# All four gate pairs of a fused Mamba and MLP block on ScalarE and GpSimd, weights loaded later, a new table of steps

## What is computed

```
x = x + mamba(layernorm(x))
x = x + mlp(layernorm(x))

mamba: xp, res = split(x @ W_in.T)              # 512 + 512 columns
       xc      = silu(causal_conv4(xp) + conv_b)
       B, C, r = split(xc @ W_x.T)              # 16 + 16 + 1 columns
       dt      = softplus(r @ W_dt.T + b_dt)    # 512 columns
       for t, for each of 16 states n:
           h[n] = exp(-A[n] * dt[t]) * h[n] + dt[t] * xc[t] * B[t, n]
       y[t]    = sum over n of h[n] * C[t, n] + D * xc[t]
       out     = silu(y + res) @ W_out.T
mlp:   h = silu((x @ w1) * s1) * ((x @ w2) * s2)      # 256 -> 1024, the "gate"
       h = gelu((h @ h1) * t1)                        # 1024 -> 1024
       h = gelu((h @ h2) * t2)                        # 1024 -> 1024
       out = (h @ w3) * s3                            # 1024 -> 256
```

## Time and profile before

| | |
|---|---|
| median of 3 runs (lowest, highest) | 2656.89 us (2654.86, 2658.69) |
| the profiled execution: its time, its span | 2656.22 us, 2654.1 us |
| busy: PE, DVE, ACT, POOL | 93%, 87%, 83%, 83% of the span |
| before scan 0 of chunk 0 | 46.7 us |
| body 0, body 1 | 81.8 us, 60.8 us |
| bodies 2 to 30 | 1740.7 us |
| body 31 and the tail up to pass B | 187 us |
| pass B | 537 us |

### The profile page before, as it was taken

One profiled execution on the slowest core, in us unless ns is written; L12 is line 12 of the kernel. 1 busy time (PEld: TensorE's weight loads), 2 busy tenths in 40 slices (PEclk: granted clock), 3 DMA queues, 4 the chain that ended last, 5 costly groups with the idle time before them and its releaser, 6 DMA issues. The chain is left out here.

```text
span 2654.1 us, 54444 instructions
## 1 busy us (share of the span) xinstructions
PE 2463.5 (93%) x18562; PEld 2237.4 (84%) x18562; DVE 2304.3 (87%) x2640; ACT 2207.4 (83%) x5264; POOL 2189.7 (83%) x1372
## 2 busy tenths in 40 slices
PE   3678999999999999999999999999977899999999
PEld 2457888888888888888888888888877899999999
DVE  1899999999999999999999999999990387677686
ACT  4799989998899999999899998999876677777774
POOL 2678999999999999999999999999975576666662
PEclk8789999999999999999999999999988899999999
DMA  6121222222222222232222222222231123222320
GB/s 240 51 63 54 73 81 73 81 77 71 79 77 76 74 76 79 70 88 69 81 73 73 77 73 81 73 81 77 68 124 68 64 96 96 96 85 92 96 96 34
DMA packets 148249, 215.91 MB, mean 81 GB/s; under 512 B 18049, under 2 KB 111361, under 8 KB 147969
## 3 DMA queue, kind: packets, MB, share of 16 engines
q1 hardware_dynamic: 147968, 212.36, 25.4%
HBM read 144.68 MB, written 50.86 MB: 74 GB/s over the span
## 5 line engine op out<-in xcount | busy, mean ns | idle before, releaser
L1499 DVE TENSOR_TENSOR_SCAN h<-banks,ub 128x512 f32<-128x512 f32 x1024 | 1196.6, 1205 | 10.4 <-POOL ub L905 3.5
L1512 DVE SCALAR_TENSOR_TENSOR acc<-banks,c_tok,acc 128x512 f32<-128x512 f32 x1024 | 714.9, 733 | 51.2 <-PE banks L1850 48.1
L1850 PE MATMUL banks<-ident,h 128*128 128x128 f32 x4096 | 623.0, 279 | 97.5 <-DVE acc L1512 51.9
L1850 PEld LDWEIGHTS banks<-ident,h 128*128 128x128 f32 x4096 | 483.5, 143 | 226.3 <-DVE h L1499 113.0
L905 POOL TENSOR_TENSOR ub<-xc_even,b_row 128x1020 f32<-128x1020 f32 x256 | 608.0, 2379 | 75.7 <-DVE h L1499 75.2
L905 POOL TENSOR_TENSOR ub<-xc_odd,b_row 128x1020 f32<-128x1020 f32 x256 | 608.1, 2379 | 53.7 <-DVE h L1499 53.1
L1292 ACT ACTIVATE banks<-dt 128x510 f32<-128x510 f32 x1024 | 607.6, 598 | 50.1 <-DVE h L1499 40.7
L1838 PE MATMUL banks<-act_high,h_rounded 128*128 128x256 f32 x2048 | 536.6, 298 | 22.1 <-POOL act_low L937 22.1
L1838 PE MATMUL banks<-act_low,h_rounded 128*128 128x256 f32 x2048 | 506.3, 283 | 0.0
L1838 PEld LDWEIGHTS banks<-act_high,h_rounded 128*128 128x128 f32 x2048 | 392.6, 192 | 28.3 <-issue 28.2
L1838 PEld LDWEIGHTS banks<-act_low,h_rounded 128*128 128x128 f32 x2048 | 393.2, 192 | 0.0
(11 more groups left out here) (167 smaller groups left out, 5784.3 us busy)
## 6 DMA issues: line engine op xcount, KB each, us to landing
b_row<-b_scratch SPq DMA_DIRECT2D x128, 512.0 KB, 4.0
z_scratch<-z_out SPq DMA_DIRECT2D x128, 256.0 KB, 2.4
zl_raw<-z_scratch SPq DMA_DIRECT2D x32, 1024.0 KB, 7.1
xp<-xp SPq DMA_DIRECT2D x128, 128.0 KB, 2.4
x_sb<-in_x SPq DMA_DIRECT2D x32, 256.0 KB, 4.3
x_res<-in_x SPq DMA_DIRECT2D x32, 256.0 KB, 2.9
h_full<-in_h SPq DMA_DIRECT2D x2, 4096.0 KB, 22.3
x_scratch<-x_sb SPq DMA_DIRECT2D x32, 256.0 KB, 2.1
```

What stands on the lines that cost most here:

```text
L1499: nc.vector.tensor_tensor_scan(h[:, n % 2, 2 * i:2 * i + 2].rearrange("p e t -> p (e t)"), banks[:, k % DECAYS, :], ub[:, n % 2, 2 * i:2 * ...
L1512: nc.vector.scalar_tensor_tensor(out=acc[:, par, q], in0=turned[q], scalar=c_tok[:, par, q, n:n + 1], in1=acc[:, par, q], op0=ALU.mult, op ...
L1850: last = nc.tensor.transpose(turned[q][:, e * P:(e + 1) * P], h[:, n % 2, e, q * P:(q + 1) * P], ident[:])
```

## The change

1. Pairs 1 and 2 of the gate go the way of 0 and 3: `BY_POOL` holds all four, `BY_DVE` none. VectorE has no work in the MLP of pass A any more.
2. SP issues the crossing of chunk 0 ahead of w1 and w2, and that of chunk 1 ahead of h2; w3 goes to step 8 of body 0.
3. Chunk 0: TensorE makes the first quarter of its B rows and the first column of B by products with the identity; VectorE and ScalarE copy them out of PSUM. VectorE does the linear part of dt (in place of ScalarE's relu), copies acc, and makes `ub[0]`. The state that enters chunk 0 is zero, so `enter`, `a_dt` and b0 are not formed there.
4. The tables of places are written anew for all engines, the pieces of checking and rounding weights too.

```diff
-        ACT_AT = dict(sums=11, x1=23, sums2=41, logs=15, logs2=41, xn=30, xp=(0, 2), silu=(6, 25), ssm=13, z=18, soft=21, acc=(28, 29), gT=14, high2=49, gg=(56, 65), high=(58, 64, 69, 69), z_out=(75, 76, 82, 86), a_dt=31)
-        POOL_AT = dict(gate=(29, 33), low2=25, x1=12, normalize=9, normalize2=21, dt=(11, 13), a_dt=15, u=(15, 15), low=(30, 32, 34, 34))
-        SP_AT = dict(crossed=(0, 0), x=0, x1=11, res=11, write_b=5, b=(9, 14, 2, 6), z_out=(36, 37, 40, 42))
+        ACT_AT = dict(sums=11, x1=22, sums2=35, logs=12, logs2=36, xn=30, xp=(0, 2), silu=(8, 25), ssm=9, z=16, soft=19, acc=(30, 30), gT=12, high2=46, gg=(55, 55, 60, 63), high=(58, 62, 63, 68), z_out=(74, 78, 85, 88), a_dt=30)
+        POOL_AT = dict(gate=(29, 29, 31, 33), low2=25, x1=12, normalize=7, normalize2=19, dt=(10, 11), a_dt=12, u=(15, 15), low=(30, 32, 34, 34))
+        SP_AT = dict(crossed=(0, 0), x=0, x1=11, res=11, write_b=4, b=(14, 15, 6, 10), z_out=(36, 38, 41, 43))
-        BY_POOL, BY_DVE = (0, 3), (1, 2)
+        BY_POOL, BY_DVE = (0, 1, 2, 3), ()
...
             load_x(1)
+            for j in range(2):
+                cross(0, j)
             for name, src in (("w1", w1), ("w2", w2)):
                 sp.dma_start(full[name][:], src.rearrange("(k p) n -> p k n", p=P)).then_inc(early_in, 16)
-            for j in range(2):
-                cross(0, j)
             write_b(0)
-            read_b(0, 0)
             read_b(0, 1)
             sp.dma_start(full["h1"][:], h1.rearrange("(k p) n -> p k n", p=P)).then_inc(h1_in, 16)
             load_x(2)
-            for name, src in (("h2", h2), ("w3", w3)):
-                sp.dma_start(full[name][:], src.rearrange("(k p) n -> p k n", p=P)).then_inc(checked_in, 16)
...
                         if n == SP_AT["crossed"][j] and to_front is not None:
                             cross(to_front, j)
+                            if to_front == 1 and j == 1:
+                                sp.dma_start(full["h2"][:], h2.rearrange("(k p) n -> p k n", p=P)).then_inc(checked_in, 16)
+                    if to_front == 1 and n == 8:
+                        sp.dma_start(full["w3"][:], w3.rearrange("(k p) n -> p k n", p=P)).then_inc(checked_in, 16)
...
+                    for e in range(ET):
+                        last = nc.vector.tensor_scalar(dt[:, 0, e], bank("dtc", 0)[:, 0:T], w_dt_sb[:, e:e + 1], b_dt_sb[:, e:e + 1], ALU.mult, ALU.add)
+                    last.then_inc(linear_done, 1)
...
+                    nc.vector.tensor_tensor(ub[:, 0, :, 1:], u[0][:, :, 1:], b_row[:, 0, 0:1, 1:].to_broadcast([P, ET, T - 1]), ALU.mult).then_inc(first_ub, 1)
...
+                            nc.tensor.matmul(turned[0][:, 0:T], select(ROW_B), ssm[:, 0], start=True, stop=True)
```

More of the change, by code:

```diff
@@ L312, in program @@
         PE_AT = dict(
[L313 to L316, removed]
@@ new lines, in program @@
+            front={1: ('conv0', 'conv1'), 5: ('ssm.a', 'ssm.b'), 11: ('dtc',), 21: ('acc0.a',), 23: ('acc0.b', 'acc0.c'), 24: ('acc1.a',), 25: ('acc1.b',), 26: ('acc1.c',)},
+            post={7: ('gT0',), 8: ('gT1',), 12: ('out.a',), 13: ('out.b',), 14: ('out.c',), 15: ('out.d',)},
+            mlp={41: ('yn',), 49: ('gg0.a', 'gg0.b'), 50: ('gg1.a', 'gg1.b'), 51: ('uu0.a', 'uu0.b'), 52: ('uu1.a', 'uu1.b', 'uu2.a'), 53: ('uu2.b', 'uu3.a', 'uu3.b', 'gg2.a'), 57: ('gg2.b',), 59: ('gg3.a', 'gg3.b'), 67: ('h0.a', 'h0.b'), 69: ('h0.c',), 70: ('h0.d',), 71: ('h1.a', 'h1.b'), 73: ('h1.c', 'h1.d'), 74: ('h2.a',), 75: ('h2.b',), 77: ('h2.c',), 79: ('h2.d',), 80: ('h3.a',), 81: ('h3.b',), 83: ('h3.c', 'h3.d')})
@@ L860, in front @@
                         nc.gpsimd.tensor_tensor(dt[:, par, rows], dt[:, par, rows], soft[:, rows], ALU.add).then_inc(dt_ready, 1)
-                if n == POOL_AT["a_dt"]:
-                    if c == 0:
+                if n == POOL_AT["a_dt"] and c >= 1:
+                    if c == 1:
                         pool.wait_ge(a_ready, 2)
@@ L902, in scan @@
                         quarter = n // QUARTER
[L903 to L906 removed]
+                        if c == 0 and quarter == 0:
+                            pool.wait_ge(rows_taken, 1)
+                        else:
+                            pool.wait_ge(b_in[quarter % 2], 16 * (2 * c + quarter // 2 + quarter % 2))
+                    if (c, n) != (0, 0):
+                        after(pool, scan_done, 2 * (NS * c + n - 1))
+                        nc.gpsimd.tensor_tensor(ub[:, n % 2, :, 1:], u[par][:, :, 1:], b_row[:, n // QUARTER % 2, n % QUARTER:n % QUARTER + 1, 1:].to_broadcast([P, ET, T - 1]),
+                                                ALU.mult).then_inc(ub_ready, 1)
                     between(n)
@@ L1130, in front @@
                     last.then_inc(soft_step, 1)
-                if n == ACT_AT["z"] + 1:
+                if n == ACT_AT["z"] + 1 and c == 0:
+                    act.wait_ge(linear_done, 1)
+                    act.sem_inc(freed("dtc", 0), 1)
+                elif n == ACT_AT["z"] + 1:
                     rows = bank("dtc", c)
@@ L1142, in front @@
                 for q in range(NT):
-                    if n == ACT_AT["acc"][q]:
+                    if n == ACT_AT["acc"][q] and c >= 1:
                         if c >= 2:
@@ L1549, in _ @@
             nothing = lambda c, n: None
-            bodies(nothing, front, scan, nothing, mlp, make_diagonals, DVE_STEPS)
+            bodies(nothing, front, scan, nothing, nothing, make_diagonals, DVE_STEPS)
             def split_rows(name, blk):
@@ L1772, in front @@
                         q = int(job[-1])
+                        if c == 0 and q == 1 and part == "a":
+                            nc.tensor.matmul(turned[0][:, 0:T], select(ROW_B), ssm[:, 0], start=True, stop=True)
+                            nc.tensor.matmul(turned[1][:, 0:NS], ssm[:, 0, 0:1].to_broadcast([P, P]), ident[:, ROW_B:ROW_B + NS], start=True, stop=True).then_inc(rows_full, 1)
                         if part != "c":
@@ L1780, in front @@
                             last.then_inc(job_full, 1)
+                            if c == 0 and q == 1:
+                                pe.wait_ge(row0_taken, 2)
+                                for r in range(1, QUARTER):
+                                    last = nc.tensor.matmul(turned[r // 2][:, r % 2 * T:r % 2 * T + T], select(ROW_B + r), ssm[:, 0], start=True, stop=True)
+                                last.then_inc(rows_full, 1)
             def post(c, n):
```

104 lines of the change are left out of this document (62 added, 42 removed).

## The result

The changed kernel takes 2691.1 us (median of 4 runs, 2688.4 to 2697.1) against 2656.7 us for the kernel before (4 runs, 2654.9 to 2658.7): ratio 1.0132, 95% interval 1.0114 to 1.0151. It is slower by 1.3%. The profiled executions have spans of 2690.2 and 2654.1 us, 36.1 apart. Forecast were 2677 us, range 2652 to 2698; the result lies inside this range, and 1 us above the narrower 2666 to 2690 of the forecast itself.

A forecast was written before the change was run, and what follows sets the result against it. VectorE was taken to bound the steady bodies, GpSimd close behind. Start -5.7, body 0 -22.2, body 1 -0.5, 29 bodies +50, body 31 -1.5, tail +1 made +21 on 2656.2: 2677 us, range 2652 to 2698.

The forecast's parts named there:

- Quarter 3: B-row read behind the third z store: GpSimd waits 0.65 us at ub[12], making bodies 61.7 us; bounds 0 and 1.5.
- the sum: Whole kernel: all terms together add 21 us to the profiled 2656.2 us, giving 2677 us.
- body 0: First body: moving chunk 1's crossing ahead of h2 removes VectorE's wait for transposes, -22.2 us, lower bound -14.
- the ending: Body 31, without a front, -1.5 us; tail, where GpSimd waits for ScalarE, +1 us, bounds -3 and +6.
- body 1: Second body: no gate there, only new places, -0.5 us.
- The bodies without that wait: Bodies 2 to 30: GpSimd's 44.45 us from ub[9] to ub[3], 16.5 to scan 7, 0.13 hand-overs: 61.1 us.
- TensorE at 0, ScalarE hidden: Steady bodies: TensorE's bank waits cost 0 (at most 1 us); ScalarE's two added scalings hide under VectorE's 4.2 us wait.
- Rival C: Steady bodies: ScalarE or the three banks become the bound, bodies of 62.7 us, 2706 us in all; chance 0.13.
- Rival B: Steady bodies: GpSimd's work packs without idle time, bodies of 58.5 us, 2583 us in all; chance 0.10.
- The start: Up to chunk 0's scan 0: earlier crossing and shorter path from u save 5.7 us, bounds -3 and -8.
- The signs: Bodies 2 to 30: VectorE near 93% busy, ub waits of 3 to 5 us a body at scans 0, 1 and 3.

The follow-up runs named there:

- e1: Changed kernel with SP's read of quarter 3 of the B rows one step earlier, ahead of the third store of z: 2657.9 us.
- e2: e1 with GpSimd gating only 16 of 256 columns of pairs 1 and 2, the others left ungated: 2648.1 us.
- e5: e2 with TensorE's acc pieces back at the places of the kernel before, the last 1.77 us earlier: 2624.4 us.
- e9: e6 with GpSimd's xT_low one step earlier, in step 8 instead of behind ub[9]: 2654.8 us.
- e11: e5 with TensorE leaving out the low part of x in the uu products: 2624.8 us.
- e7: e1 with three ub buffers, one z buffer, one factor in pass B's last scaling, dt a step later, acc at old places: 2630.8 us.
- e12: e9 with the gate of pair 2 alone back on VectorE, in step 14: 2650.1 us.
- e6: e1, gates whole, with TensorE's acc pieces back at the places of the kernel before, the last 1.77 us earlier: 2655.3 us.

## Why the forecast was right, and where it was not

**The stretch.** Set beside each other, from the start of ub[15] to the start of scan 3 (one body of each profile), and what is left of a body:

| kernel | ub[15] to scan 3 | body | rest |
|---|---|---|---|
| before | 1019.94 to 1040.44, 20.5 | 60.0 | 39.5 |
| changed kernel | 1020.35 to 1041.70, 21.4 | 62.2 | 40.8 |
| e1 | 1003.13 to 1024.56, 21.4 | 61.0 | 39.6 |
| e2 | 1001.61 to 1023.12, 21.5 | 60.9 | 39.4 |
| e5 | 991.59 to 1011.93, 20.3 | 60.1 | 39.8 |
| e9 | 1002.12 to 1023.49, 21.4 | 61.0 | 39.6 |
| e11 | 989.94 to 1010.28, 20.3 | 60.1 | 39.8 |
| e7, three ub buffers | 991.95 to 1013.33, 21.4 | 60.1 | 38.7 |
| e12 | 1003.52 to 1024.47, 21.0 | 61.1 | 40.1 |

The rest is VectorE's ten steps from scan 3 to scan 13 (35.5), a last scan (2.3), and waits, or, before, a gate pair (0.88). Before, and in e1, e2, e5, e9 and e11, it hardly changes, and the body follows the stretch. It is 1.2 us more in the changed kernel, whose wait for quarter 3 lies ahead of ub[15], and less in e7, where ub[15] need not wait for scan 13. That the rest stayed at 39.6 from before to e1 hides two changes that cancel: a gate pair of VectorE went, and the wait for the transposes of step 10 came. Before, ub[15] stood ahead of a_dt (0.34) and u:

```profile
1019.94 2.36 POOL L905 TENSOR_TENSOR ub<-xc_odd,b_row 128x1020 f32<-128x1020 f32 x1
1022.25 0.34 POOL L865 TENSOR_TENSOR a_dt<-dt,neg_a 128x64 f32<-128x64 f32 x1
```

Now the gate of pair 2 (1.24 from start to start) stands there in place of a_dt (0.29): +0.95 us. In the mean of the bodies the stretch grew by 0.86 us and the body by 0.95 (e1).

**Point by point.**
- Quarter 3: the mechanism was right, the size not. In the mean of the 28 bodies with the wait the read was issued 7.8 us after scan 7 (forecast 7.5), took 4.24 us to land (forecast 4.0), and GpSimd asked for it 10.9 us after scan 7 (forecast 10.8). The 4.0 was the median of all b_row reads; those of quarter 3 alone took 4.22 us before as well, so the store ahead of the read did not lengthen it. The body shown above, with 5.3 us to landing, is the worst one. The wait is 1.19 us in the mean of 29 bodies, not 0.65: 15.5 us more, as much as the sum fell short (+21 forecast, +36 measured). The other misses cancel: body 0 and the ending 4.1 us worse, the bodies without this wait and body 1 5 us better.
- The bodies without that wait: forecast 61.1, measured 60.97 (e1). The length that I gave to ub[9] up to ub[3], 44.45 us, is 44.38 in e1 (980.14 to 1024.52), and GpSimd has no hole in it. So the chain that I forecast is there, but it is not the only one: at ub[15] GpSimd is tied to the recurrence as well (before, 1019.94, 0.13 us behind the end of scan 13; in e1 0.15), and I didn't look for a second tie. The two are of nearly one length, and that the first alone gave the right number is in part luck. e9 shows it: a piece taken from the first half of the stretch is worth nothing, where my working gives it up to 1.28 us.
- "TensorE at 0, ScalarE hidden": the number held, the slack behind it did not. TensorE's acc, moved half a step later, would cost as much as the gate, and is hidden behind it (e2, e5, e6). The new wait for the transposes of step 10 eats what VectorE was spared on its way to scan 13, and so keeps the second tie. Rival C, ScalarE and the banks, doesn't set the bodies of the changed kernel; in e11, at 60.1 us, TensorE waits for ScalarE's silus instead.
- Rival B (GpSimd's work packs) was priced at 58.5 us. With a third buffer GpSimd is busy for 58.3 us of a body (e7), but the body is 60.07: part of the difference is what it waits for ScalarE and TensorE at xn and a gate (33 us in 29 bodies); what else holds it was not tested.
- The start: -5.8 for -5.7, closer than it could be known: in the profiles of the kernels with this start, scan 0 of chunk 0 begins anywhere from 39.1 to 41.1 us. Body 0: -20.0 for -22.2; a wait of 3.45 us for transposes was left that I had not counted. Body 1: -1.9 for -0.5. The ending: +1.4 for -0.5.
- VectorE's busy time fell by 1.4 us a body, not by the 1.7 of two gate pairs; nothing in the sum hung on it.
- The signs came true: VectorE busy 92.5% in bodies 2 to 30, waits for ub of 3.05 us a body at scans 0, 1 and 3, and no wait of GpSimd for the recurrence in steps 10 to 15.

Where the gain went: VectorE's 1.4 us less of work a body became idle time, ahead of scans 0, 1 and 3 and at the transposes of step 10; the start's 28 us were kept, and paid for more than twice by the 29 bodies, 35 us by quarter 3 and 27 by the stretch.

What stays open: what holds e5, e7 and e11 at 60.1 us. In e5 it is the same stretch by the table, with 0.25 us of gate left and VectorE's 1.07 us wait for transposes in the rest; in e11 TensorE had less work, and the wait moved from step 10 to step 11. No run took this wait away without another in its place, none spread TensorE's products otherwise, and none put the gate of pair 2 into steps 5 to 9, where GpSimd waits for the recurrence 2.3 us a body. A kernel with the new start, whole gates and a body below 60 us wasn't found.

## What to carry to other kernels

Before work is moved to an engine with free time, look for where that time lies: with two buffers between producer and consumer, only the steps in which the producer waits can take work, and each point at which it is released by the consumer cuts its chain anew. Find the last such point before the consumer waits. As long as the consumer itself comes to that point no sooner (here a wait of 1.0 us for transposes kept it late), only what stands behind the point costs, and what is taken away ahead of it brings nothing. When an edit that should help does nothing, look for a second wait of the same length at the same place (here the gate and acc1) and take away both.
